# A four-layer graph network on one core: layer 1 attends before it projects, and its logits come from dot products on VectorE

## The reference

```python
# layer 0: degree and neighbour sum
out = deg * (h @ Wi.T + b) + a @ (h @ Wj.T)
# layer 1: one-head graph attention
Wh = h @ W;  e_src = Wh @ a_src;  e_dst = Wh @ a_dst
logits = leaky_relu(e_src[:, None] + e_dst[None, :], 0.2)
attn = softmax(where(adj == 0, -inf, logits));  out = attn @ Wh
# layer 2: the same with F1 = 128 and a finite mask; out = concat(alpha @ h2, h2)
# layer 3: 8 heads of 32
q, k, v = h @ Wq.T + bq, h @ Wk.T + bk, h @ Wv.T + bv
out = softmax(mask(q k^T / sqrt(32))) v @ Wo.T + bo
```

## Time and profile before

| | before |
|---|---|
| median of 3 runs | 1220.35 us |
| profiled execution | 1220.8 us, span 1218.8 us, granted clock 0.999 |
| PE busy | 1200.7 us (99%) |
| DVE busy | 1053.9 us (86%) |
| ACT busy | 1082.4 us (89%) |
| POOL busy | 1068.4 us (88%) |
| DMA | 78.57 MB, mean 64 GB/s |

### The profile page before, as it was taken

How to read it: one execution, slowest core, us unless ns; L and a number is a source line. 1 busy time by engine, 2 the same in 40 slices (tenths; PEclk the granted TensorE clock), 3 DMA queues, 4 the chain that set the end, 5 groups by cost and what they waited for, 6 DMA issues and landing times.

```text
span 1218.8 us, 43750 instructions
## 1 busy us (share of the span) xinstructions
PE 1200.7 (99%) x12017; PEld 1108.6 (91%) x12017; DVE 1053.9 (86%) x5142; ACT 1082.4 (89%) x3976; POOL 1068.4 (88%) x1848
## 2 busy tenths in 40 slices
PE   8999999999999999999999999999999999999997
PEld 7789999999999999999999999999999999999986
DVE  6898898898898898888988988988988888988874
ACT  3679898898898898898998998998998998998997
POOL 5998899899899898999899899899899899898774
PEclk9999999999999999999999999999999999999999
DMA  7333333343442433534333332432433343330001
GB/s 187 63 46 51 77 68 55 79 67 57 77 67 57 77 67 55 79 64 60 77 63 60 77 65 58 75 68 59 71 69 60 69 67 66 67 51 26 20 20 36
DMA packets 97678, 78.57 MB, mean 64 GB/s; under 512 B 31648, under 2 KB 89248, under 8 KB 97440
## 3 DMA queue, kind: packets, MB, share of 16 engines
q1 hardware_dynamic: 94960, 74.07, 32.9%
q10 hardware_dynamic: 2480, 1.71, 0.5%
HBM read 58.79 MB, written 16.95 MB: 62 GB/s over the span
## 4 chain that ended last, share of the span: by engine, by line
PE 90%; issue 1%; DVE 1%; POOL 0%; ACT 0%; POOLq 0%; DVEq 0%; ACTq 0%
PE bank L1565 16%; PE bank L1567 16%; PE bank L1566 16%; PE bank L1715 9%; PE bank L1670 6%; PE bank L1575 6%; PE bank L1707 6%; PE bank L1727 5%; PE bank L1646 4%; PE bank L1662 3%; PE bank L1626 2%; POOL probs L469 0%; ACT exps L1315 0%; DVE masked L874 0%; PE bank L1654 0%
## 5 line engine op out<-in xcount | busy, mean ns | idle before, releaser
L1315 ACT ACTIVATE exps<-masked,nmax 128x128 f32<-128x128 f32 x1024 | 396.8, 393 | 0.9 <-DVE nmax L874 0.4
L469 POOL TENSOR_TENSOR probs<-exps,rsum 128x512 f32<-128x512 f32 x256 | 266.3, 1042 | 16.2 <-DVE rsum L882 15.7
L440 POOL TENSOR_SCALAR y<-x,nm,rstd 128x256 f32<-128x256 f32 x384 | 212.0, 560 | 31.5 <-issue 31.0
L874 DVE CUSTOM_DVE_ANT_0 masked<-bank,mask 128x128 f32<-128x128 f32 x1024 | 227.4, 284 | 0.8 <-PE bank L1707 0.5
L1315 ACT ACTIVATION_READ_ACCUMULATOR exps<-masked,nmax 128x1 f32 x1024 | 197.3, 193 | 0.0
L760 DVE BATCH_NORM_STATS2 stats<-x 128x6 f32<-128x256 f32 x512 | 190.4, 414 | 4.6 <-DMA x<-in_x 4.4
L1565 PE MATMUL bank<-w_hi,ht_hi 128*128 128x512 f32 (+1 forms) x508 | 189.4, 373 | 0.4 <-DVE ht_lo L821 0.3
L417 POOL TENSOR_TENSOR rstd<-veps,power 128x2 f32<-128x2 f32 x256 | 182.7, 714 | 5.3
L1567 PE MATMUL bank<-w_hi,ht_lo 128*128 128x512 f32 (+1 forms) x508 | 172.6, 340 | 0.0
L1566 PE MATMUL bank<-w_lo,ht_hi 128*128 128x512 f32 (+1 forms) x508 | 172.5, 340 | 0.0
L1323 ACT ACTIVATE probs3t<-bank 128x512 f32<-128x512 f32 x256 | 145.0, 595 | 0.7 <-PE bank L1715 0.7
(11 more groups left out here) (136 smaller groups left out, 3970.4 us busy)
## 6 DMA issues: line engine op xcount, KB each, us to landing
x<-in_x SPq DMA_DIRECT2D x64, 256.0 KB, 5.9
xt_sb<-in_xt SPq DMA_DIRECT2D x64, 256.0 KB, 5.7
out<-x SPq DMA_DIRECT2D x64, 256.0 KB, 5.7
db<-rows SPq DMA_DIRECT2D x110, 128.0 KB, 4.1
mean_b<-rows SPq DMA_DIRECT2D x62, 128.0 KB, 3.4
rows<-dst SPq DMA_DIRECT2D x110, 1.0 KB, 3.6
rows<-mv SPq DMA_DIRECT2D x62, 1.0 KB, 5.8
probs<-in_w0t ACTq DMA_DIRECT2D x1, 256.0 KB, 3.5
```

The source lines that it names most:

```text
L440: last = pool.tensor_scalar(y[i][:, b, g], src[:, bx, g], nm[i][:, s, g:g + 1], rstd[i][:, s, g:g + 1], ALU.add, ALU.mult)
L469: pool.tensor_tensor(probs3[:, p % BUFFERS["probs3"], j], exps3[:, p % BUFFERS["exps3"], j], rsum3[:, s, j].unsqueeze(2).to_broadcast([P, ...
L874: last = dve.tensor_tensor_reduce(masked3[:, b, j, i], bank_of(f"sc{j}")[:, i * P:(i + 1) * P], mask[:], scale=-1.0, scalar=-MASKED, op0=A ...
L1315: last = act.activation(exps3[:, b, j, i], masked3[:, p % BUFFERS["masked3"], j, i], ACT.Exp, bias=nmax3[:, s, j, i:i + 1], scale=-1.0, ac ...
```

## The change

- Layer 1 is reordered. POOL `centre1` makes y1 = relu(x1 - mean), not scaled by rstd. DVE `logit_products1` takes four dot products a pair (two graphs by two vectors) of y1 with W a_src and W a_dst, which `multiply_weights` now lays out as rows on all partitions in PSUM bank 6 (`a1_rows`), kept for the whole run. POOL `scale_logits1` multiplies by rstd. The e_dst row goes to DRAM straight from there; `gather_dst` is for layer 2 alone.
- The exponentials are transposed as before; ACT copies them out per graph with the node's rstd as scale. PE `aggregate1` then forms the transposed aggregate (attn @ h) of both graphs with y1 as weights (4 f32 products of 128 columns), ACT and DVE split it in high and low (`high_g1`, `low_g1`), and `project1` multiplies by W (12 products of 256 columns) straight into the bank that `sum_x2` reads.
- Gone: `transpose_y(1)`, `relu_transposed_high/low` of layer 1, `copy_projection1`, `attend(1)`, `gather_dst(1)`.
- x1 and y1 get 3 buffers for 2; bank 6 leaves the rotation, so 6 banks go round.
- `add_bias` of the key stays on DVE. LAG, BANKS and all lists are redrawn; PE's loop goes over 60 steps as before, from lag -2 to 7 where it was -1 to 7.

The core of the diff:

```diff
+        a1_rows = bank[6]
...
 
-            def write_row(i, p):
+            def write_row1(p):
                 b, q = p % 2, p - BY_TRANSPOSE[0]
-                sp.wait_ge(S[f"dst{i}"], q + 1)
+                passed(sp, "sd1", p)
                 if q >= 2:
-                    sp.wait_ge(row_in[i][b], q // 2 * 16)
-                sp.dma_start(rows[i][b], dst[i][:, b]).then_inc(row_out[i][b], 16)
+                    sp.wait_ge(row_in[1][b], q // 2 * 16)
+                sp.dma_start(rows[1][b], logits1[:, p % SMALL, 1]).then_inc(row_out[1][b], 16)
+
+            def write_row2(p):
+                b, q = p % 2, p - BY_TRANSPOSE[0]
+                sp.wait_ge(S["dst2"], q + 1)
+                if q >= 2:
+                    sp.wait_ge(row_in[2][b], q // 2 * 16)
+                sp.dma_start(rows[2][b], dst2[:, b]).then_inc(row_out[2][b], 16)
...
             def inverse_deviation(i, p):
                 b = p % SMALL
                 passed(pool, f"veps{i}", p)
+                if i == 1:
+                    passed(pool, "at1", p, SMALL)
...
+            def centre1(p):
+                b, s, bx = p % BUFFERS["y1"], p % SMALL, p % BUFFERS["x1"]
+                passed(pool, "nm1", p)
+                read_before(pool, "y1", p, "dots1", "g1_mm")
+                for g in range(G):
+                    last = pool.tensor_scalar(y[1][:, b, g], x1[:, bx, g], nm[1][:, s, g:g + 1], 0.0, ALU.add, ALU.max)
+                last.then_inc(S["y1"], 1)
+
+            def scale_logits1(p):
+                s = p % SMALL
+                passed(pool, "dots1", p)
+                passed(pool, "rstd1", p)
+                passed(pool, "z1", p, SMALL)
+                pool.tensor_tensor(logits1[:, s], dots1[:, s], rstd[1][:, s].unsqueeze(1).to_broadcast([P, 2, G]), ALU.mult).then_inc(S["sd1"], 1)
...
                 dve.wait_ge(S["products"], 1)
                 dve.wait_ge(adjacency, 7)
                 for c in range(DC):
-                    last = dve.tensor_copy(w1_sb[:, c, D:D + 2], bank_of("prep")[:, P + 4 * c:P + 4 * c + 2])
-                last.then_inc(w1_whole, 1)
-                for c in range(DC):
                     dve.tensor_copy(w2_sb[:, c, F1:F1 + 2], bank_of("prep")[:, P + 4 * c + 2:P + 4 * c + 4])
                 dve.scalar_tensor_tensor(c3[:], bank_of("prep")[:, D:2 * D], nan_row[:], c3[:], ALU.add, ALU.add).then_inc(c3_made, 1)
-                dve.wait_ge(w1_whole, 1)
                 dve.tensor_copy(w1_r[0][:], w1_sb[:]).then_inc(w1_high, 1)
                 dve.wait_ge(w1_high, 1)
                 dve.tensor_tensor(w1_r[1][:], w1_sb[:], w1_r[0][:].bitcast(F32), ALU.subtract).then_inc(S["w1_split"], 1)
...
+            def logit_products1(p):
+                b, s = p % BUFFERS["y1"], p % SMALL
+                passed(dve, "y1", p)
+                dve.wait_ge(S["products"], 1)
+                passed(dve, "dots1", p, 1)
+                passed(dve, "sd1", p, SMALL)
+                for g in range(G):
+                    for k in range(2):
+                        last = dve.tensor_tensor_reduce(products1[:, k, g], a1_rows[:, k * D:(k + 1) * D], y[1][:, b, g], scale=1.0, scalar=0.0,
+                                                        op0=ALU.mult, op1=ALU.add, accum_out=dots1[:, s, k, g:g + 1])
+                last.then_inc(S["dots1"], 1)
+
+            def low_g1(p):
+                b = p % BUFFERS["ht1"]
+                passed(dve, "g1_hi", p)
+                read_before(dve, "ht1", p, "x2_mm")
+                dve.tensor_tensor(ht1_r[1][:, b].rearrange("p c g n -> p (c g n)"), bank_of("g1")[:],
+                                  ht1_r[0][:, b].rearrange("p c g n -> p (c g n)").bitcast(F32), ALU.subtract).then_inc(S["g1_lo"], 1)
...
-            def copy_projection1(g, p):
-                b = p % BUFFERS["wh"]
-                passed(act, f"wh{g}_mm", p)
-                read_before(act, "wh", p, "x2_mm", "z1")
-                act.activation(wh[:, b, g], bank_of(f"wh{g}")[:, 0:D + 2], ACT.Copy).then_inc(S[f"wh{g}"], 1)
+            def high_g1(p):
+                b = p % BUFFERS["ht1"]
+                passed(act, "g1_mm", p)
+                read_before(act, "ht1", p, "x2_mm")
+                act.activation(ht1_r[0][:, b].rearrange("p c g n -> p (c g n)"), bank_of("g1")[:], ACT.Copy).then_inc(S["g1_hi"], 1)
+
+            def copy_exp_transposed1(p):
+                b, s = p % BUFFERS["at1"], p % SMALL
+                passed(act, "e1t", p)
+                passed(act, "rstd1", p)
+                read_before(act, "at1", p, "g1_mm")
+                for g in range(G):
+                    last = act.activation(at[1][:, b, g], bank_of("at1")[:, g * P:(g + 1) * P], ACT.Copy, scale=rstd[1][:, s, g:g + 1])
+                last.then_inc(S["at1"], 1)
...
+                for k in range(2):
+                    for e in range(DC):
+                        pe.matmul(a1_rows[:, k * D:(k + 1) * D], a1_sb[:, e, k:k + 1].to_broadcast([P, P]), w1t_sb[:, e, :], start=(e == 0), stop=(e == DC - 1))
                 for c in range(DC):
-                    for e in range(DC):
-                        pe.matmul(bank_of("prep")[:, P + 4 * c:P + 4 * c + 2], w1t_sb[:, e, c * P:(c + 1) * P], a1_sb[:, e, :],
-                                  start=(e == 0), stop=(e == DC - 1))
...
 
-            def project1(g, p):
+            def aggregate1(p):
+                b, bt = p % BUFFERS["y1"], p % BUFFERS["at1"]
+                passed(pe, "at1", p)
+                bank_free(pe, "g1", p)
+                for c in range(DC):
+                    for g in range(G):
+                        last = pe.matmul(bank_of("g1")[:, (c * G + g) * P:(c * G + g + 1) * P], y[1][:, b, g, c * P:(c + 1) * P], at[1][:, bt, g],
+                                         start=True, stop=True)
+                last.then_inc(S["g1_mm"], 1)
+
+            def project1(p):
                 b = p % BUFFERS["ht1"]
-                passed(pe, "h1t_lo", p)
+                passed(pe, "g1_lo", p)
                 pe.wait_ge(S["w1_split"], 1)
-                bank_free(pe, f"wh{g}", p)
-                for c in range(DC):
-                    last = split_matmul(bank_of(f"wh{g}")[:, 0:D + 2], [h_[:, b, c, g] for h_ in ht1_r], [w_[:, c, :] for w_ in w1_r],
-                                        c == 0, c == DC - 1)
-                last.then_inc(S[f"wh{g}_mm"], 1)
+                bank_free(pe, "x2b", p)
+                for g in range(G):
+                    for c in range(DC):
+                        last = split_matmul(bank_of("x2b")[:, g * D:(g + 1) * D], [h_[:, b, c, g] for h_ in ht1_r], [w_[:, c, :] for w_ in w1_r],
+                                            c == 0, c == DC - 1)
+                last.then_inc(S["x2_mm"], 1)
...
```

More of the change, by code:

```diff
@@ L368, in _ @@
             fill()
-            for t in range(17, NP + 12):
+            for t in range(18, NP + 14):
                 step(t)
@@ L559, in fill @@
+                negative_mean(1, "y1", 5)
+                shifted_variance(0, 7)
+                normalise(2, x2, 2)
+                centre1(5)
+                x3_tail(1)
+                shifted_variance(1, 5)
+                clear_empty_rows(3)
+                inverse_deviation(1, 5)
+                subtract_means(7)
+                inverse_deviation(0, 7)
+                scale_logits1(5)
+                biased_x0(8)
                 shifted_variance(3, 1)
@@ L701, in _ @@
             fill()
-            for t in range(9, NP + 4):
+            for t in range(3, NP - 1):
                 step(t)
@@ L960, in fill @@
+                mask_logits(1, mask, 2)
+                add_own(1, 4)
+                mean_and_variance(1, 3)
+                low_mj(1, 4)
+                low_mj(0, 4)
+                stats_of(0, x0, 7)
                 sum_x2(1)
-                relu_difference_low(4)
+                mean_and_variance(0, 7)
                 stats_of(2, x2, 1)
+                relu_difference_low(5)
                 mean_and_variance(2, 1)
+                add_own(0, 4)
+                logit_products1(3)
@@ L992, in fill @@
-                mean_and_variance(0, 7)
-                add_own(0, 5)
-                mask_logits(1, mask, 3)
+                sum_x1(5)
+                mean_and_variance(2, 2)
+                relu_transposed_low(3, ht3_r, last_of("kt_mm", "qt_mm", "v_mm"), 0)
+                inverse_sum(1, "rsum1_any", "x2", 3)
+                stats_of(1, x1, 5)
+                low_mj(1, 6)
+                mean_and_variance(1, 5)
+                low_mj(0, 6)
+                mask_logits(2, mask2, 1)
+                add_own(1, 6)
@@ L1194, in _ @@
             fill()
-            for t in range(11, NP + 6):
+            for t in range(10, NP + 6):
                 step(t)
@@ L1769, in fill @@
                 transpose_exp(1, 1)
+                project1(0)
+                spread_dst(1, logits1[:, (2) % SMALL, 1], "sd1", 2)
+                aggregate(3)
+                aggregate1(1)
+                project0(1, 4)
```

(17 more changed lines are left out.)

1124 lines of the change are left out of this document (521 added, 603 removed), and 26 rows, old and new, of the table LAG.

## The result

The changed kernel takes 1242.4 us (median of 4 runs, 1242.0 to 1243.0) beside 1220.7 us of the kernel before on the same chip: a ratio of 1.018, interval 1.016 to 1.0196. The forecast was 1203 us, faster. It is slower by 21.7 us.

The account below looks back on a forecast made before the run. PE, busy all of its 18.38 us step, was taken as the bound: minus 0.40 of its work, plus 0.12 coupling, gives 18.10; over 64 steps minus 17.9 us, plus 0.5 at the ends, 1203 us, range 1189 to 1222.

Parts of the forecast that it names:

- `centre1` has the two operations of `normalise`. Net about 0: 16.7 busy: POOL's step: gather_dst(1) goes, scale_logits1 comes, centre1 priced like normalise; 16.7 us busy, 17.2 with issue gaps, below PE.
- the dot products: DVE's new logit_products1: four per pair at 0.34 us each, 1.38 together; bounds 0.84 and 2.0.
- such a circle: DVE and PE as two circles of nearly one length, 18.0 us for DVE's, meeting several times a step.
- Ends: Fill and end of the run, with a pair one step deeper in flight: plus 0.5 us, bounds minus 5 to plus 8.
- the step of 18.10: Forecast time per pair in the middle: PE's 17.98 us plus 0.12 of coupling, against 18.38 before.
- the coupling of 0.12: Small delays between PE and DVE no longer made up: 0.12 us a step, bounds 0 and 0.40.
- the 0.40 of the sum: PE's net saving per step: transpose_y(1) gone (0.44 us), aggregate1 for attend(1) plus 0.04; PE step 17.98.
- Whole length: Rival at logit_products1: dot products without overlap, 0.50 us each, DVE's circle 18.6, 1235 us; chance 0.16, including any DVE step over 18.4.
- Bank 1: Rival: DVE reaches sum_x3 late, PE's scores wait each step; step 18.3 to 18.4, 1216 to 1221 us; chance 0.14.
- The late e_dst row: Rival: SP's transfers and queue add 1.5 us, ACT waits at sum_logits; step 18.3, 1215 us; chance 0.10.
- Coupling 0: Rival: the change does only what it takes off PE; step 17.98, 1195 us; within the forecast's 0.60 for coupling 0 to 0.25.
- POOL without a gap: Sign that the forecast is wrong: POOL's list running with no idle time; no size given.

Follow-up runs that it names:

- e2: Changed kernel with centre1's maximum with 0.0 replaced by a product with 1.0, leaving out layer 1's relu: 1216.6 us.
- e12: e6 with POOL's r (x3 plus bias, 1.28 us) moved behind x3_tail and head 1's probabilities, three x3 buffers for two: 1229.5 us.
- e5: Changed kernel with centre1 done by ACT (Relu with the negative mean as bias) instead of POOL: 1248.8 us.
- e9: e5 plus the means' row of pair 10 written early, with ACT's layer 3 head 0 exponentials moved behind its copy of hh: 1301.6 us.
- e6: Changed kernel with one DMA moved in SP's opening list: pair 10's means written before pair 4's layer 2 destination row: 1237.2 us.
- e10: Changed kernel with the product for the maximum, the means' row written early and dot products over half the features: 1210.5 us.
- e14: e13 with pair 0's projection on PE ahead of two layer 0 products of pair 3, and DVE's x2 of pair 0 earlier: 1315.6 us.
- e15: e13 with pair 0's projection on PE put later, behind layer 0's aggregate of pair 3: 1310.9 us.
- e18: e14's opening change on the changed kernel with the product for the maximum (no layer 1 relu) and the means' row early: 1217.7 us.
- e1: Changed kernel with centre1's maximum taken against a column of zeros instead of the immediate 0.0: 1252.6 us.
- e13: e12 without POOL's negative means: centre1 and the two normalisations subtract the mean itself: 1311.0 us.
- e17: Changed kernel with the means' row early and centre1's second graph of every pair on DVE instead of POOL: 1268.0 us.

## Why the prediction was wrong

**The step that failed: "`centre1` has the two operations of `normalise`. Net about 0: 16.7 busy".** It has the same number of operations on the same shape, but another pair of them. They cost 2.29 us for the pair of graphs where the row taken as their price has 1.10. That row, from the page of the kernel before:

```profile
L440 POOL TENSOR_SCALAR y<-x,nm,rstd 128x256 f32<-128x256 f32 x384 | 212.0, 560 | 31.5 <-issue 31.0
```

POOL's step became 17.7 instead of 16.7. With the quick pair in its place (e2) the step was 18.10, the value forecast. The prediction bounded the dot products from both sides because their shape was missing in the trace; `centre1`, whose pair of operations was missing too, got one row's price and no bounds. The other near row, `x3_tail`'s addition of two tensors of 128x256 at 0.68, would have given only a quarter of a microsecond more for the pair: no row of before showed 1.15. What was lacking is the rival in which `centre1` is dear, with the point from which POOL decides. With the right price the prediction's own sum for POOL, 17.9 busy and 0.5 of gaps, would already have stood above 18.10.

**And cover was judged by totals.** POOL with 17.7 busy of 18.46 still has slack in its column. The circle of 8.2 us of DVE and 10.3 of POOL has none. Of the 0.36 us between 18.10 and 18.46, e12 puts 0.17 down to the circle, by moving one operation across its edge (7.7 us in all), and 0.19 to POOL's list as a whole. e5 and e9 moved work to ACT, which has the most idle time, and lost. The prediction did look for such a circle, but between DVE and PE.

**Ends, "I take plus 0.5", bounds minus 5 to plus 8.** With the quick pair (e2) the step is as forecast, and 13.7 us of the measured time, 1216.6 less 1202.9, are in the ends and the opening, above the bound of 8: the first scores came 8.5 us late, and SP's order cost 5.2 us more. The second is shown (e6): that means stand behind a late row in SP's queue, which the prediction counted for the steps ("behind the wait for the row's landing stand the next means and loads"), it left out of the opening. Of the first scores' lateness, x2 of pair 0 is 8.7 us late already (42.65 against 33.92 us) and the first scores are late by as much. Its cause is open. Half the dot products (e10) move nothing; the chain of pair 0 moved in e14 and e15 and the first scores did not follow, under a slower POOL; e18 failed to move it. What the rows show is a PE with less to do in 22 to 45 us, busy 19.48 us before, 14.95 in e2, with a granted clock of 0.93 and 0.85. That stretch in e2 (columns as in the earlier trace rows):

```profile
22.00:45.00 23.00, 14.95 (x70) 11.39 (x71) 19.86 (x78) 11.26 (x32) 20.72 (x34) 0.85 0.51 100
```

And in the kernel before:

```profile
22.00:45.00 23.00, 19.48 (x104) 15.62 (x105) 19.54 (x61) 13.04 (x35) 21.01 (x34) 0.93 0.58 88
```

Layer 1's projection, which PE had there, now needs the softmax first; that this is the cause is argued, not shown.

**The account.** Measured less forecast is 39 us: 25.8 the maximum (e2), 6.1 the row's place with half dot products (e10 against e2), 7.1 the rest, in the main the late opening (1210.5 against 1203.4).

**What was right.** The dot products: 0.345 apart, 0.34 forecast; DVE's step 17.8, 17.70 forecast. `aggregate1`: 0.90. ACT: 16.3.

**Right by luck: the step of 18.10.** e2 and e10 have it, but not by the coupling of 0.12 between PE and DVE: taking 0.54 us a step from DVE (e10) left the step where it was, with every other engine waiting. So PE's saving was 0.28, not the 0.40 of the sum, and the coupling of 0.12, which no run shows, stood in its place. Which of PE's groups holds the difference is open.

**The rivals.** *Whole length*: refuted by the starts, 0.345 us apart for 0.421 long. The Trainium skill, "VectorE: DVE Perf Modes", section "The DRAIN you can't avoid", says that the next operation does not start until the pipe has emptied, which by itself would have them 0.42 apart or more, and that one that is not held starts earlier; the rows fit the latter. *Bank 1*: PE waits for `sum_x3` once from 200 to 1100 us, for 0.2 us; refuted. *The late e_dst row*: ACT's `sum_logits` waits for it once from 200 to 1100 us, 0.5 us; refuted. *Coupling 0*: its 17.98 was not reached, but its mechanism is the one that e10 bears out, with a PE step of 18.1. The time came out above the range, on the slower side that had 0.16, by none of the mechanisms named. Of the signs listed for wrong, "POOL without a gap" was the one that came nearest: 0.75 us idle of 18.46, where 1.7 were before.

## What to carry to other kernels

An operation whose exact form isn't in the trace has no price in the trace: same engine, same shape and same number of operands were not enough, the pair of operations decided a factor of two. And an engine's idle share doesn't say that work may be put there. Follow the chain from a waiting instruction back around to itself; if it closes within one step's length, what is added to it is added to the step, and what is taken from it comes off the step until the next bound is reached (here POOL's list, 18.29). Moving an operation across its edge can pay though no work goes: 7.7 us in e12.

## What the runs showed of the hardware

`tensor_scalar` with two operations, 128x256 f32, SBUF to SBUF, on POOL: addition and product 478 ns (one column, one immediate; e2) or 557 (two columns; the changed kernel); addition and maximum 1152 (the changed kernel) or 1230 (e1); subtraction and product 1229 (two columns; e13); subtraction and maximum 1143 (one column; e13). The 128 of the changed kernel's `centre1` all lie between 1140 and 1160 ns, whatever the other engines do. Why the pairs differ is not shown.

Addition and maximum on VectorE takes 326 ns at its quickest and 1382 in the median, ending with the POOL operation beside it (e17). The Trainium skill, "SBUF — State Buffer", section "Who interferes with whom", says that VectorE's two-port mode and GpSimd take a shared pair of ports in turn, each for a whole instruction, so that the other waits. The rows of e17 agree: 1.41 us beside a POOL operation of 1.29 that began 0.04 us earlier, and 1.44 us for POOL's where VectorE's began 0.07 us earlier. That this instruction ran in the two-port mode, the rows do not show.
